# First attention: spread norms in one row, chunk products in one run, softplus behind the first moments

## What is computed

```python
q, k, v = silu(conv4(x @ q_w)), silu(conv4(x @ k_w)), silu(conv4(x @ v_w))
beta = sigmoid(x @ b_w)
q, k = l2norm(q), l2norm(k)              # per head
kb, vb = k * beta, v * beta              # chunks of 32 tokens
A = -strict_lower(kb @ k.T)              # one 32 x 32 matrix per chunk and head
T = inverse(I - A); u, w = T @ vb, T @ kb
for chunk in 32 chunks:                  # the recurrence
    attn = lower(q @ k.T); u_hat = u - w @ S
    o = q @ S + attn @ u_hat; S = S + k.T @ u_hat
branches = [conv1(v), conv3(v), conv7(v), conv31(v), o, v]
stats = mean, std, mean|.|, norm of each branch and head
weights = softmax(mlp(x, stats) / (softplus(gate_log_temp) + 0.5))
out = rmsnorm(sum(weights * branches)) @ o_w
```

## Time and profile before

| | us |
|---|---|
| median of 3 runs | 952.9 |
| the runs | 949.75, 952.9, 954.26 |
| the profiled execution | 950.6 |
| its span | 949.3 |
| mean granted PE clock | 0.894 |

### The profile page before, as it was taken

How to read it: one execution, slowest core, us unless ns; L and a number is a source line. 1 busy time by engine, 2 the same in 40 slices (tenths; PEclk the granted TensorE clock), 3 DMA queues, 4 the chain that set the end, 5 groups by cost and what they waited for, 6 DMA issues and landing times. The chain is left out here.

```text
span 949.3 us, 17691 instructions
## 1 busy us (share of the span) xinstructions
PE 760.2 (80%) x6704; PEld 327.7 (35%) x6704; DVE 672.4 (71%) x1319; ACT 509.2 (54%) x1003; POOL 244.3 (26%) x297
## 2 busy tenths in 40 slices
PE   6889958887419999946887999999999999628880
PEld 3323236543315676724111222222222222215660
DVE  7857975458783434338786999999999998653545
ACT  4733512465403333344336888888888888404433
POOL 0130010314035666560651200000100000025643
PEclk9989979989658999977758999999999999858995
DMA  3520000000461111131876030321300000151113
GB/s 92 130 49 3 1 23 4 4 2 0 176 202 40 42 44 42 40 102 39 228 159 197 2 80 2 80 43 39 79 2 2 3 2 11 24 227 42 42 31 94
DMA packets 40618, 57.62 MB, mean 61 GB/s; under 512 B 12424, under 2 KB 27920, under 8 KB 39768
## 3 DMA queue, kind: packets, MB, share of 16 engines
q1 hardware_dynamic: 36568, 48.36, 18.9%
q0 software_dynamic: 3968, 8.13, 3.0%
HBM read 37.54 MB, written 14.75 MB: 55 GB/s over the span
## 5 line engine op out<-in xcount | busy, mean ns | idle before, releaser
L983 DVE TENSOR_REDUCE arena<-psum 128x1 f32<-128x1024 f32 x256 | 301.0, 1217 | 23.6 <-PE psum L877 20.9
L1113 ACT ACTIVATE arena<-psum 128x512 f32<-128x512 f32 x512 | 266.8, 604 | 57.0 <-PE psum L894 56.9
L877 PE MATMUL psum<-arena 56*128 56x512 bf16 x512 | 181.2, 413 | 10.6 <-DVE arena L983 8.8
L894 PE MATMUL psum<-arena 59*128 59x512 bf16 x512 | 157.9, 390 | 7.8 <-ACT arena L1113 6.1
L905 PE MATMUL psum<-arena 128*32 128x512 f32 x1024 | 138.1, 611 | 8.7 <-issue 8.7
L894 PEld LDWEIGHTS psum<-arena 59*128 59x128 bf16 x512 | 38.3, 94 | 172.0 <-ACT arena L1113 149.1
L473 POOL DMA_INDIRECT rows_y<-arena x62 | 61.8, 997 | 64.8 <-DVE arena L424 61.8
L381 PEld LDWEIGHTS psum<-arena 128*128 128x128 f32 x496 | 62.8, 192 | 40.2 <-issue 28.4
L381 PE MATMUL psum<-arena 128*128 (+1 forms) x496 | 66.9, 278 | 11.9 <-ACT arena L452 11.9
L372 PE MATMUL psum<-arena 128*128 x124 | 68.4, 635 | 2.8 <-DVE arena L409 2.7
L468 POOL DMA_INDIRECT arena<-rows_x,arena x62 | 60.3, 972 | 35.4 <-issue 17.0
(11 more groups left out here) (304 smaller groups left out, 1126.1 us busy)
## 6 DMA issues: line engine op xcount, KB each, us to landing
arena<-scr_k SPq DMA_DIRECT2D x15, 448.0 KB
arena<-scr_q SPq DMA_DIRECT2D x15, 448.0 KB
arena<-in_f_up SPq DMA_DIRECT2D x1, 4096.0 KB, 13.8
arena<-rows_y SPq DMA_DIRECT2D x12, 256.0 KB, 5.0
scr_q<-arena SPq DMA_DIRECT2D x6, 384.0 KB, 3.8
arena<-in_f_down SPq DMA_DIRECT2D x1, 2048.0 KB, 20.0
rows_x<-xn SPq DMA_DIRECT2D x2, 1024.0 KB, 17.0
arena<-in_f_up SPq DMA_DIRECT2D x1, 2048.0 KB, 8.4
```

The source lines that it names most:

```text
L877: mm = pe.matmul(ps[:, bank + half, :], q[rows, k, h, (qh * 4 + qt) * P:(qh * 4 + qt + 1) * P], kk[rows, k, h, half * BLK:(half + 1) * BLK ...
L894: pe.matmul(ps[:, n % 3, :], kk[0:KA, k, h, kb * P:(kb + 1) * P], q[0:KA, k, h, qh * BLK:(qh + 1) * BLK], start=True, stop=True).then_inc( ...
L983: dve.tensor_reduce(mx[:, qh, h * 4 + qt:h * 4 + qt + 1], ps[:, bank:bank + 2, :].rearrange("p a b -> p (a b)"), X, ALU.max).then_inc(S("a ...
L1113: act.activation(pt[:, (u % 3) * HG + h, :], ps[:, n % 3, :], ACT.Exp, scale=float(HD) ** -0.5).then_inc(S("a1_exp"), 1)
```

## The change

Three moves and nothing else; no instruction of work is added or taken out.

- ACT: the softplus (wait, Exp, wait, Ln) becomes a function, called for block 0 between the fourth `moments` and the copy of the third filter.
- PE: the norms 4 and 5 follow norm 3 behind step 2. Norms 6 and 7 stand behind the first statistics unit (branch 5 of block 0).
- PE: all 16 product groups stand behind step 3, the first step of the third filter of block 0.

```diff
     g0 = m["a0_tt"][:, 0, :]
-    act.wait_ge(S("a0_g0"), 1)
-    act.activation(g0, g0, ACT.Exp).then_inc(S("a0_softplus"), 1)
-    act.wait_ge(S("a0_softplus"), 1)
-    act.activation(g0, g0, ACT.Ln, bias=1.0).then_inc(S("a0_softplus"), 1)
+
+    def softplus():
+        act.wait_ge(S("a0_g0"), 1)
+        act.activation(g0, g0, ACT.Exp).then_inc(S("a0_softplus"), 1)
+        act.wait_ge(S("a0_softplus"), 1)
+        act.activation(g0, g0, ACT.Ln, bias=1.0).then_inc(S("a0_softplus"), 1)
+
...
         moments(k + 3, 0, n)
+        if n == 0:
+            softplus()
         filtered(n, 2)
...
         if step == 2:
-            for u in range(4):
+            for u in range(6):
                 shared(u)
-        if step == 5:
-            shared(4)
-            shared(5)
-        if step == 6:
-            shared(6)
-            shared(7)
-        if 9 <= step < 13:
-            for n in range(4 * step - 36, 4 * step - 32):
+        if step == 3:
+            for n in range(B * GR):
                 products(n)
...
                 statistics(k + 2 * (i - 1) + j, s, n, s == 5, False)
+                if n == 0 and s == 5:
+                    shared(6)
+                    shared(7)
```

## The result

| | before | after |
|---|---|---|
| median of six runs, us | 951.71 (945.28 to 954.26) | 941.95 (939.42 to 944.73) |
| ratio of the two, 95% interval | | 0.9907 (0.9887 to 0.9927) |
| the profiled execution | 950.6 | 941.9 |
| its span | 949.3 | 940.6 |
| first spread to the recurrence's first matmul | 86.2 | 75.9 |

The change is worth 9.8 us of the median. The profiled pair gains 8.7 us: 10.3 in the stretch that was edited and 1.1 in the recurrence, less 1.5 in the outputs, 0.5 behind them, and 0.7 that this trace already lies behind at its first spread (47.80 us, where before had it at 47.08). In what follows 0.72 us is taken off a time of after wherever it is set beside a time of before or of the prediction.

The account below looks back on a forecast made before the run. DVE's chain up to the recurrence was taken as the bound, passing to the filters' end. Recurrence 10.2 us earlier plus 0.7 from clock makes 10.9: 939.7 against the profiled 950.6, predicted as 941.0, range 934.5 to 946.5.

Parts of the forecast that it names:

- fourth spread: Spread norm u = 3 on PE, waiting for ACT's second filter copy: starts at 49.64 instead of 51.27 us.
- second block's run of eight: Second block's eight filter steps on PE: begin at 82.5 instead of 84.25 us, 1.8 us earlier.
- last sum ready: Branch sums, the recurrence's other condition: ready at 123.1 instead of 124.88 us, later than DVE's 121.7.
- The waits: DVE's waits for norms disappear, ending them at 55.7, 9.2 us earlier; PE waits 1.5 us for the last norm.
- Abs behind Exp: On ACT, Abs directly behind the norms' Exp may need a table load: 0 to 1.28 us, taken as 0.
- The product run: 1024 records on PE, limited by instruction blocks at 69 records a us: 12.6 us, bounds 7.7 to 14.9.
- head start: Product records passing beyond the 69 a us that arrive: 156, from 534 against 378 in today's products.
- Rival (a): Instructions arrive fast enough, DVE's products end at 65.7: 14.4 us gained in all, 936 to 938 us; chance 0.15.
- The change of sides: Filters' end at 123.1 replaces DVE's 121.7 as the recurrence's bound, losing 1.4 us of DVE's gain.
- What the shorter idle gives back: First three chunks of the recurrence at full PE clock after a gap under 1 us: 0 to 1.4, taken 0.7 us.
- Everything behind follows the recurrence: Stages after the recurrence's start at 133.31 us simply move earlier with it; no separate gain or loss priced.
- Rival (b): PE's clock falls in the product run, slowing the filter steps behind: 942.7 to 944.4 us; chance 0.17.

Follow-up runs that it names:

- doubled: Changed kernel with every chunk product made twice into the same place, 2048 records instead of 1024: 960.33 us.
- two more filter steps ahead (and zeros): Changed kernel with product groups 0 to 2 behind step 4, 3 to 15 behind step 5, and matmuls of zeros in the two gaps before the spreads: 941.55 us.
- products spread: Changed kernel with the product groups back behind filter steps 9 to 12, four each: 944.8 us.
- softplus back: Changed kernel with the softplus back in its old place on ACT: 947.86 us.
- run alone: Kernel before with only the products moved, all 16 groups in one run behind step 6, norms and softplus as they were: 939.24 us.
- one pass: Changed kernel with chunk products reading only the upper 16 bits of q, k and kb as bf16, half the matmuls and weight loads: 935.85 us.
- two steps later: Changed kernel with product groups 0 to 2 behind step 4 and 3 to 15 behind step 5, without zeros: 941.39 us.

## Why the prediction was right

941.0 us was predicted, with 934.5 to 946.5; 941.95 was measured. Step by step, with 0.72 taken off the times of after:

| step | predicted | measured |
|---|---|---|
| first filter's copy | 47.40 | 47.41 |
| fourth spread | 49.64 | 49.66 |
| DVE through with the norms | 55.7 | 55.8 |
| first product | 55.9 | 55.96 |
| group 3 | 58.7 | 58.8 |
| length of the product run | 12.6 | 12.4 |
| DVE through with the products | 69.2 | 68.8 |
| solved | 121.7 | 121.7 |
| second block's run of eight | 82.5 | 82.3 |
| last sum ready | 123.1 | 122.9 |
| recurrence begins | 123.1 | 123.0 |

**The waits.** The prediction walked two in-order lists forward with durations from before's rows, and every step of this table came out within 0.4 us. Two terms beside it did not, and cost nothing. PE waited 0.69 us for the last norm and not 1.5, because spreads, statistics and the filter step lasted until 55.3 and not 54.4; that was idle time anyway. And the solve, taken as fixed at 52.5 us, took 52.9 (69.52 to 122.46): that DVE had solved at just 121.7 is an early start of 0.4 us and a solve 0.4 longer. Abs behind Exp cost nothing, the end of its bounds that was taken.

**The product run.** The term with the widest bounds (7.7 to 14.9 us) was the one that instruction supply decides. It is shown, not only argued: halving the records removes the stops, doubling them adds 15.4 us with a stop at each 256 records, and the stops stay when the clock is held. The DMA records of the traces agree: the instruction queue moves packets of 16,384 bytes, one to each stop. In after they start at 62.13 and 65.60 us and the stops end at 64.47 and 67.92, 2.3 us behind each; in the doubled kernel each of the seven stops ends 2.4 to 2.9 us behind the start of its packet, and the next packet starts 1.0 to 1.1 us after the stop. The weight loads of after show the same blocks:

```profile
64.47 1.83 PEld L2136 LDWEIGHTS psum<-arena 32*32 32x32 f32 x128 [1.62 <-issue]
67.92 0.97 PEld L2136 LDWEIGHTS psum<-arena 32*32 32x32 f32 x65 [1.62 <-issue]
```

The term came out by two errors that cancel. Here a block took 3.45 us, 74 records a us instead of 69; of the 1024 records 12.38 x 74 = 916 arrived during the run, which leaves a head start of 108 instead of 156. Rival (a) falls with this. The Trainium skill ("Runtime: NRT & Kernel Launch", Instruction fetch mechanics) has the block's size right by these rows, 256 instructions; that the fetch is hidden does not hold for a run of small matmuls, where it costs 1.46 us a block here and up to 2.01 in the doubled run.

**The change of sides.** The recurrence is released by ACT's last sum, 1.1 us behind DVE. The kernel with two more filter steps ahead (and zeros) turns the releaser back to DVE.

**What the shorter idle gives back: not shown.** 0.7 us was taken, and the recurrence is 1.1 shorter (64.2 to 63.1), at a clock of 1.00 instead of 0.94. PE is busy 2.0 us less in it (55.24 to 53.26), so the clock's gain did not arrive in full. TensorE starves at 130.08 already, 6.4 us into the loop, where before it first did so 17.7 us into it, at 151.03.

```profile
130.08 0.40 PE L2264 MATMUL psum<-arena 32*32 32x96 f32 x9 [0.46 <-issue]
133.84 0.44 PE L2264 MATMUL psum<-arena 32*32 32x96 f32 x10 [0.31 <-issue]
137.61 0.45 PE L2264 MATMUL psum<-arena 32*32 32x96 f32 x12 [0.30 <-issue]
```

These stops end 3.76 and 3.77 us apart, the interval of the prediction (3.71). But that the 1.1 us come from the shorter idle does not follow. The kernel with the products spread keeps before's idle time (9.06 us) and its low clock over the first 6.9 us of the loop, and its recurrence is shorter than after's (columns of the earlier trace rows):

```profile
129.90:192.50 62.60, 55.13 (x2101) 40.64 (x2101) 29.98 (x192) 23.93 (x91) 11.03 (x13) 0.94 0.02 4
```

Taken from its first matmul to the first one behind it, the recurrence lasts 63.9 us in before, 62.3 in that kernel, 62.8 in after and 60.0 to 64.0 in the other variants of after, with none of its instructions changed. A difference of 1 us between two traces lies within that.

**What was missing: the outputs, -1.5 us.** "Everything behind follows the recurrence" was wrong by this. The windows show the same work with PE's busy time up from 34.98 to 36.27 us and the clock down from 0.86 to 0.83; DVE, ACT and POOL are busy as long as before. The two kernels in which this stage ran at 0.72 (softplus back) and 0.70 (run alone) took 54.4 and 54.9 us in it, so its length goes with the clock. When the clock falls there was not predicted and is not explained by these runs. The thirteen other traces have 0.70 to 0.83 there, the run-alone kernel's among them, and before's 0.86 is a single trace, so it is not shown either that the change is what costs the 1.5 us. These two differences (+0.4 and -1.5), with 0.5 behind the attention and the 0.7 ahead of the first spread, are the difference between 939.7, the sum against the profiled execution, and its 941.9.

**Rival (b), the clock, did not happen in after but is real.** The clock stayed at 1.00 to the recurrence in both traces of the changed kernel. In five variants of it and in the run-alone kernel it fell, at 49.9 to 52.4 us. Where the products of such a variant stand right behind that, they start 2.1 us later (one pass, doubled) or, with the softplus back as well, 4.9. Four of them (products spread, one pass, two steps later, doubled) have exactly after's instructions on TensorE up to there. The window of 52 to 58 us in after:

```profile
52.00:58.00 6.00, 5.32 (x121) 2.24 (x116) 6.00 (x10) 3.56 (x6) 5.37 (x5) 1.00 0.25 55
```

and in the kernel with each product twice:

```profile
52.00:58.00 6.00, 6.00 (x28) 1.10 (x20) 6.00 (x9) 2.01 (x4) 5.05 (x5) 0.50 0.19 41
```

Ahead of it PE had been idle for 0.83 us, busy for 1.14 and idle for 1.44 in both (for after, the first two rows of its timeline). Why it fell in one and not in the other stays open. The six runs of after lie within 5.3 us of each other, so it may well have fallen in some of them; the profiles can't tell. It fell in four of the six traces with these instructions and gaps, so the chance of 0.17 for this rival was rather too low, and that it held in both traces of after is luck for the forecast as far as these runs show.

## What to carry to other kernels

Where many small matmuls stand in a row, count TensorE's records (matmuls and weight loads, two of each for an f32 matmul) and set them against the rate at which blocks of instructions arrive: here 256 in 3.5 to 4.0 us, so that 133 records a us could be executed and about 70 arrive. Fewer records then help where a further change of order did not: one pass took the run from 12.4 to 6.3 us, and two filter steps moved ahead of the products gained nothing. When a stage has two conditions, walk both lists forward through the new order before pricing it: 1.1 us behind the old bound stood the new one, and moving work between the two ends bought nothing more. And price a small move through everything that waits behind it, the clock of TensorE included, and not at its own length: 1.6 us of ACT were worth 2.8 to 5.1, by how TensorE's clock stood in the trace that it is set against. Where the clock differs between single traces, a stage's gain or loss of 1 to 3 us is not yet the change's.

## What the runs showed of the hardware that was not expected

- The block interval is not one number: 3.45 us in after, 3.45 to 4.00 within the doubled run, and 3.7 to 4.0 in the kernel with products two steps later. In the product run the stops stand exactly 256 records apart and behind the same records of TensorE's list, counted from its first, in after, softplus back, two steps later, doubled and run alone (942 and 1198 are common to all five), so an edit that puts other records ahead of the products shifts where in the run they fall.
- The same instructions with the same gaps ahead of them left TensorE at 2.4 GHz (1.00) in one kernel and at 1.2 GHz (0.50) in another. A gap of 3.06 us was followed by the lower level in all three kernels that have it; one of 1.44 us in four of the six traces that have it.
